# Second loop of an eight-layer kernel: the next pair's residual input prepared one iteration ahead

## The reference

```python
x = x + _L0_attn_ref(_layernorm(x), ...)   # cosine-weighted attention and an MLP
x = x + _L0_ffn_ref(_layernorm(x), ...)    # channel mix with the token before
x = x + _L1_attn_ref(_layernorm(x), ...)   # latent attention
x = x + _L1_ffn_ref(_layernorm(x), ...)    # two groups of 32 experts, 2 chosen in each
x = x + _L2_attn_ref(_layernorm(x), ...)   # rotary causal attention, 16 heads
x = x + _L2_ffn_ref(_layernorm(x), ...)    # 8 experts, 2 chosen
x = x + _L3_attn_ref(_layernorm(x), ...)   # state-space layer (Mamba), gated RMS norm
x = x + _L3_ffn_ref(_layernorm(x), ...)    # attention among the heads of a token, soft experts
```

## Time and profile before

| | |
|---|---|
| median of 3 runs | 5831.26 us (5829.92 to 5835.9) |
| profiled execution, its time | 5804.77 us |
| its span | 5803.2 us |
| second loop | from 2543.4 us to 5661.5 us of the span |
| busy PE, DVE, POOL, ACT | 4503.4, 3665.5, 2279.9, 1757.0 us |
| mean granted TensorE clock | 0.862 |

### The profile page before, as it was taken

The page is one execution under the profiler, slowest core; times in us unless marked ns, Lnnn a source line. Parts: engine busy times, 40 slices in busy tenths (PEclk is TensorE's granted clock), DMA queues, the critical chain, the costliest instruction groups (busy, mean ns, idle before and its releaser), DMA issues. The chain is left out here.

```text
span 5803.2 us, 89650 instructions
## 1 busy us (share of the span) xinstructions
PE 4503.4 (78%) x33608; PEld 2606.0 (45%) x33608; DVE 3665.5 (63%) x10873; ACT 1757.0 (30%) x2749; POOL 2279.9 (39%) x2754
## 2 busy tenths in 40 slices
PE   5979788797979795958778688787786786877872
PEld 4454445454544443634535435445354354453442
DVE  4565656565656563647586685676765956757665
ACT  2424243333333342423232241232322422413220
POOL 3333333333342334445253271362533623614435
PEclk9989899898989897968888888888888888888885
DMA  3000000000000004720000000000000000000000
GB/s 119 8 16 12 13 13 13 15 11 16 10 20 6 19 7 159 231 72 2 16 14 5 18 8 10 21 2 16 14 5 16 10 9 20 4 13 17 5 14 4
DMA packets 141739, 145.74 MB, mean 25 GB/s; under 512 B 31112, under 2 KB 126026, under 8 KB 140770
## 3 DMA queue, kind: packets, MB, share of 16 engines
q1 hardware_dynamic: 114130, 93.01, 5.5%
q0 software_dynamic: 18432, 37.79, 2.3%
q10 hardware_dynamic: 8736, 8.91, 0.5%
HBM read 69.17 MB, written 62.59 MB: 23 GB/s over the span
## 5 line engine op out<-in xcount | busy, mean ns | idle before, releaser
L815 DVE CUSTOM_DVE_ANT_0 twin<-twin,w_mask_row 128x512 f32<-128x512 f32 (+3 forms) x2048 | 951.5, 522 | 335.4 <-PE twin L1777 333.9
L1777 PE MATMUL twin<-arena 32*128 32x128 f32 (+3 forms) x4096 | 803.5, 519 | 38.9 <-DMA arena<-hres 16.7
L1795 PE MATMUL twin<-arena 32*128 32x128 f32 (+3 forms) x4096 | 792.6, 505 | 33.7 <-DVE arena L815 32.1
L1723 PE MATMUL twin<-w_ident_b 128*128 128x512 bf16 x1536 | 455.1, 449 | 390.3 <-DVE mv L775 158.6
L1450 ACT ACTIVATE arena<-twin 128x768 f32<-128x768 f32 (+1 forms) x544 | 479.3, 881 | 686.6 <-PE twin L1806 387.5
L705 POOL TENSOR_SCALAR ve<-mv 128x4 f32<-128x4 f32 x128 | 27.5, 214 | 1458.9 <-DVE mv L775 1458.3
L1795 PEld LDWEIGHTS twin<-arena 32*128 32x128 f32 x4096 | 348.3, 199 | 479.4 <-issue 289.2
L328 POOL DMA_INDIRECT got<-sorted_y,back x288 | 280.8, 975 | 540.4 <-ACT ring L1657 290.5
L1723 PEld LDWEIGHTS twin<-w_ident_b 128*128 128x128 bf16 x1536 | 155.9, 111 | 660.3 <-DVE mv L775 182.1
L1777 PEld LDWEIGHTS twin<-arena 32*128 32x128 f32 x4096 | 356.9, 206 | 198.1 <-issue 111.2
L320 POOL DMA_INDIRECT sorted_x<-got,w_mo_first_slots x288 | 287.0, 997 | 97.9 <-issue 56.0
(11 more groups left out here) (422 smaller groups left out, 9473.4 us busy)
## 6 DMA issues: line engine op xcount, KB each, us to landing
sorted_y<-arena SPq DMA_DIRECT2D x96, 256.0 KB, 2.8
sorted_x<-zeros ACTq DMA_DIRECT2D x2, 4096.0 KB, 19.9
a<-sorted_x SPq DMA_DIRECT2D x64, 128.0 KB
b<-sorted_x SPq DMA_DIRECT2D x64, 128.0 KB, 2.5
hres<-sorted_x SPq DMA_DIRECT2D x64, 128.0 KB
sorted_x<-got,w_mo_first_slots POOLq DMA_INDIRECT x288
got<-sorted_y,back POOLq DMA_INDIRECT x288, 2.6
x_out<-w_l_w SPq DMA_DIRECT2D x18, 256.0 KB, 2.3
```

The source lines that it names most:

```text
L815: last = dve.tensor_tensor_reduce(s[:, e, at:at + w], s[:, e, at:at + w], W["mask_row"][:, T - w:T], -1.0, 3e38, ALU.add, ALU.min, into)
L1723: pe.matmul(into, ident_b, ident_b.unsqueeze(1).broadcast_to([P, NT, P]), start=True, stop=True, skip_group_check=True)
L1777: last = pe.matmul(s[:, e, at:at + w], queries[r, P * i:P * (i + 1)], keys[r, 0:w], start=(at == 0), stop=True, skip_group_check=True)
L1795: last = pe.matmul(s[:, e, at:at + w], keys[r, P * m:P * (m + 1)], queries[r, P * m:T], start=(at == 0), stop=(tag == "l2"), skip_group_ch ...
```

## The change

The next pair's residual input gets a buffer of its own, `XN[q]`, and the head of an iteration is moved into the end of the one before.

- SP no longer loads X at the start of an iteration. It loads `XN[q]` for the next pair once DVE has read the present one (`l2_moved`, after the attention). `kept_x` gets one more row for the index of the iteration after the last.
- The additions (`add_chosen`, the same 16 instructions for each q) are cut into four steps and placed by hand: steps 0 to 2 of q = 0 before the wait for the output projection, the rest, both statistics and both norms into `l3_front` around the two `take_queries`. Every iteration does them, the last too, whose result nobody uses.
- The expert section does them for the first pair, behind its row fetches.
- ACT's four fills move from the head to the start of `l3_front` (`clear_rows`), and into the expert section for the first iteration.
- POOL's fetches are two after each `l3_xc`, two after each of four and one after each of four more `l3_decay` signals, none in the head front. It makes the two scales at the end of the iteration.
- PE's `keep_busy` at the head of the iteration is gone, and its turns wait for nothing.
- `back`, the table of rows and weights, is loaded at once at the start, no longer behind the additions.

```diff
+        XN = pair_sb("x_next", [P, NT, D])
...
+        def add_chosen(dve, sg, q, steps):
+            for c in steps:
+                k, g = divmod(c, GROUPS)
+                if c == 0:
+                    dve.wait_ge(sg[f"x_loaded{q}"], 16)
+                    dve.wait_ge(sg[f"m_got{q}"], 16 * SLOTS_OF_SEQ)
+                else:
+                    dve.wait_ge(sg[f"m_adding{q}"], c)
+                for t in range(NT):
+                    n = NT * GROUPS * k + GROUPS * t + g
+                    i = dve.scalar_tensor_tensor(XN[q][:, t], got[q][:, n],
+                                                 back[:, q, SLOTS_OF_SEQ + n:SLOTS_OF_SEQ + n + 1], XN[q][:, t],
+                                                 ALU.mult, ALU.add)
+                i.then_inc(sg[f"m_adding{q}"], 1)
+                if c == ADDS - 1:
+                    dve.wait_ge(sg[f"m_adding{q}"], ADDS)
+        def clear_rows(act, q):
+            act.activation(at_k4[q], ...)      # ones
+            return act.activation(at_q4[q], ...)   # zeros
...
 # expert section, DVE (POOL makes the two scales, ACT clears the rows)
+                        for q in PAIR:
+                            add_chosen(dve, sg, q, range(ADDS))
+                            ... statistics of XN[q] ...
+                        for q in PAIR:
+                            dve.wait_ge(sg["rstd_ready"], q + 1)
+                            ... A[q] = norm of XN[q] ...
...
 # second loop, SP
-                        for q in PAIR if first < LAYERS else ():
-                            src = (x_in[...] if first == 0 else kept_x[bass.ds(pair + 1, 1), q])
+                        for q in PAIR if first == 0 else ():
+                            src = x_in[...]
                             sp.dma_start(X[q][:], src).then_inc(sg[f"x_loaded{q}"], 16)
...
-                            sp.wait_ge(sg[f"l2_rows_clear{q}"], 2)
...
+                        for q in PAIR if first <= L2_ATTENTION < last else ():
+                            src = kept_x[bass.ds(pair + 2, 1), q]...
+                            sp.wait_ge(sg["l2_moved"], q + 1)
+                            sp.dma_start(XN[q][:], src).then_inc(sg[f"x_loaded{q}"], 16)
...
 # POOL
-                                        fetch_rows(pool, sg, (4 + m,))
+                                        fetch_rows(pool, sg, (4 + 2 * m, 5 + 2 * m))
...
-                                        fetch_rows(pool, sg, (12 + 2 * m, 13 + 2 * m))
+                                        fetch_rows(pool, sg, (20 + 2 * m, 21 + 2 * m) if m < 4 else (24 + m,))
...
-                                if layer == LAYERS - 1:
-                                    fetch_rows(pool, sg, (28 + 2 * of_layer, 29 + 2 * of_layer))
...
 # DVE
                         def l2_attention():
-                            for q in PAIR:
-                                add_experts(q)
-                                layernorm_stats(q)
-                            for q in PAIR:
-                                layernorm_apply(q, "l2_a")
...
-                                done(dve.tensor_tensor(X[q][:], X[q][:], l2_bo, ALU.add))
+                                dve.tensor_tensor(X[q][:], XN[q][:], l2_bo, ALU.add).then_inc(sg["l2_moved"], 1)
...
                                 rms_apply(q, ma_y[q], ma_y[q], "l3_y")
+                            add_chosen(dve, sg, 0, range(0, ADDS - 1))
                             for q in PAIR:
                                 dve.wait_ge(sg["l3_out_mm"], q + 1)
...
+                            add_chosen(dve, sg, 0, range(ADDS - 1, ADDS))
+                            layernorm_stats(0, XN)
+                            add_chosen(dve, sg, 1, range(0, 2))
+                            take_queries(0)
+                            layernorm_apply(0, "l2_a", src=XN)
+                            add_chosen(dve, sg, 1, range(2, ADDS))
+                            layernorm_stats(1, XN)
+                            take_queries(1)
+                            layernorm_apply(1, "l2_a", src=XN)
...
 # ACT
-                            fill(at_k4[0], 1, "l2_rows_clear0")
-                            fill(at_q4[0], 0, "l2_rows_clear0")
-                            fill(at_k4[1], 1, "l2_rows_clear1")
-                            to_f(0, "l2_turn", 1, "l2_f", b=3)
-                            fill(at_q4[1], 0, "l2_rows_clear1")
-                            to_f(1, "l2_turn", 2, "l2_f", b=3)
+                            for q in PAIR:
+                                to_f(q, "l2_turn", q + 1, "l2_f", b=3)
...
                         def l3_front():
+                            for q in PAIR:
+                                act.wait_ge(sg["l3_out_mm"], q + 1)
+                                clear_rows(act, q)
...
 # PE
                         def l2_attention():
-                            keep_busy(pb(0, 3), ("m_added", 1), ("stats_ready", 1), ("m_added", 2), ("stats_ready", 2))
                             for q in PAIR:
-                                turn(q, A[q], "l2_a", q + 1, "l2_turn", b=3)
+                                turn(q, A[q], None, 0, "l2_turn", b=3)
```

More of the change, by code:

```diff
@@ L329, in fetch_rows @@
                                         bass.IndirectOffsetOnAxis(ap=back[:, q, n:n + 1].bitcast(U32), axis=0)
-                                        ).then_inc(sg["m_got"], 16)
+                                        ).then_inc(sg[f"m_got{q}"], 16)
+        def add_chosen(dve, sg, q, steps):
[15 more added lines that the diff above has]
+        def clear_rows(act, q):
+            act.activation(at_k4[q], W["l2_rope_k"].unsqueeze(1).broadcast_to([P, HG, T]), ACT.Identity,
+                           bias=W["ones"][:, 0:1], scale=0.0)
+            return act.activation(at_q4[q], W["l2_rope_k"].unsqueeze(1).broadcast_to([P, HG, T]), ACT.Identity,
+                                  bias=0.0, scale=0.0)
         for first, last in PARTS:
@@ L466, in _ @@
                                                ).then_inc(sg["e_silu"], 1)
+                        act.wait_ge(sg["e_w"], 2 * UNITS)
+                        for i in range(3):
+                            act.wait_ge(sg[f"e_stored{i}"], 16 * (UNITS // 3))
+                        for q in PAIR:
+                            clear_rows(act, q)
                     @block.vector
@@ L547, in _ @@
                         dve.tensor_copy(back[:], ex_back[:, 2:4]).then_inc(sg["e_first_back"], 1)
+                        for q in PAIR:
+                            add_chosen(dve, sg, q, range(ADDS))
+                            for t in range(NT):
+                                i = dve.bn_stats(BS[q][:, t], XN[q][:, t])
+                            done(i)
+                            for t in range(NT):
+                                i = dve.bn_aggr(MV[q][:, t], BS[q][:, t])
+                            i.then_inc(sg["stats_ready"], 1)
+                        for q in PAIR:
+                            dve.wait_ge(sg["rstd_ready"], q + 1)
+                            for t in range(NT):
+                                dve.tensor_scalar(A[q][:, t], XN[q][:, t], MV[q][:, t, 0:1], RS[q][:, t:t + 1],
+                                                  ALU.subtract, ALU.mult)
                 clear_signals()
@@ L555, in _ @@
                     def _(sp):
-                        for q in PAIR if first < LAYERS else ():
-                            src = (x_in[bass.ds(pair, 1), q] if first == 0 else kept_x[bass.ds(pair + 1, 1), q]
-                                   ).rearrange("b (t p) d -> p (b t) d", p=P)
+                        for q in PAIR if first == 0 else ():
+                            src = x_in[bass.ds(pair, 1), q].rearrange("b (t p) d -> p (b t) d", p=P)
                             sp.dma_start(X[q][:], src).then_inc(sg[f"x_loaded{q}"], 16)
@@ L1367, in l3_front, with take_queries @@
                                                        W["l3f_bo"].unsqueeze(1).broadcast_to([P, NT, D]), ALU.add))
-                            for q in PAIR:
+                            def take_queries(q):
                                 dve.wait_ge(sg["f_q_mm"], q + 1)
@@ L1583, in l2_attention @@
                         def l2_attention():
-                            def fill(rows4, value, ready):
-                                act.activation(rows4, W["l2_rope_k"].unsqueeze(1).broadcast_to([P, HG, T]), ACT.Identity,
-                                               bias=W["ones"][:, 0:1] if value else 0.0, scale=0.0
-                                               ).then_inc(sg[ready], 1)
-                            fill(at_k4[0], 1, "l2_rows_clear0")
-                            fill(at_q4[0], 0, "l2_rows_clear0")
-                            fill(at_k4[1], 1, "l2_rows_clear1")
-                            to_f(0, "l2_turn", 1, "l2_f", b=3)
-                            fill(at_q4[1], 0, "l2_rows_clear1")
-                            to_f(1, "l2_turn", 2, "l2_f", b=3)
```

(6 more changed lines are left out.)

63 lines of the change are left out of this document (30 added, 33 removed).

## The result

The change takes the median from 5830.59 to 5778.94 us, four runs each on one chip: ratio 0.991, 95% interval 0.989 to 0.9929. The forecast was 5776, in a range of 5750 to 5808.

A forecast was written before the change was run, and what follows sets the result against it. It took the serial chain at each turn between iterations, 28.4 us from last work to first scores, as the bound. Seven turns 53.9 plus first iteration 4.4 minus last 3.3 gave 55 us, median 5831.3 to 5776, range 5750 to 5808.

The forecast's parts named there:

- the clock term: Turn to first scores: without keep-busy PE starts at 1.2 GHz, costing 2.5 us a turn, bounds 0 to 5.
- DVE's wait for the load: Head of the iteration: DVE idles 103.4 us in eight waits for X to arrive, 12.9 us an iteration.
- turn behind the start of PE's branch: Loop turn: PE's turn of q = 0 starts 3.8 us after its branch began instead of 17.3, removing 13.5 us.
- DVE's tail behind ACT: Iteration's end: DVE ends at 2939.0 against ACT's 2935.75, so the turn comes 3.3 us later.
- saved in a turn: Each of seven turns with a branch back: 13.5 - 3.3 - 2.5 = 7.7 us saved, 53.9 in all.
- twelve additions under the output projection: DVE before the output projection's wait: 3.5 us of additions hidden in 3.80 us of idle time, no cost.
- first iteration, last fetch to scores: Entry without a branch: first scores at 2565.1 instead of 2569.56, 4.4 us saved.
- A low clock that drags on: Attention: five or more of eight iterations lose 3.5 us, 18 to 28 us, giving 5794 to 5804; chance 0.17.
- slower by the same mechanism: Low clock lasts further into iterations; 19 us more each eats the gain, 30 gives 5862 us; chance 0.07.
- The larger saving: Turn: short branch and no clock cost give 5730 us; long branch without clock cost 5759; chance 0.16.
- Nothing changes: Turn: uncovered additions (3.5), longer branch (1.4) and low clock throughout (2.5) take 7.4 of 7.7 us, 5831; chance 0.05.
- The profiled time: Whole profiled execution: forecast to go from 5804.8 to 5750 us.

The follow-up runs named there:

- e8: Changed kernel with the twelve additions of q = 0 moved from before the output projection's wait into `l3_front`; ratio 0.9936 to the kernel before, 5747.32 us.
- e6: Changed kernel with two pairs in one step of the second loop, three branches back instead of seven; ratio 0.986 to the kernel before, 5709.82 us.
- e5: Changed kernel with keep-busy matmuls added at the end of PE's `l3_front`; ratio 0.9909 to the kernel before, 5737.04 us.
- e3: Kernel before without the keep-busy matmuls at the head of the second loop's iterations; ratio 1.0036 to the kernel before, 5857.65 us.
- e4: Changed kernel run again, unchanged; ratio 0.987 to the kernel before, 5768.2 us.
- e11: Changed kernel run a third time, unchanged; ratio 0.9898 to the kernel before, 5726.64 us.
- e2: Kernel before with only the next pair's residual input loaded one iteration ahead into its own buffer; ratio 0.9954 to the kernel before, 5813.07 us.
- e10: e7 with all eight pairs written out, no branch back in the second loop; ratio 0.9793 to the kernel before, 5672.10 us.
- e9: e7 with two pairs in one step of the second loop; ratio 0.9799 to the kernel before, 5668.35 us.
- e7: Changed kernel with q = 0 additions moved into the last four scan steps, q = 1's before the output projection's wait; ratio 0.9857 to before, 5699.43 us.
- e1: Kernel before run again, unchanged; ratio 1.0, 5837.46 us.

## Why the prediction was right

Its mechanism held step by step for the turn, and so did the sum. Two things in it were not as told: what the clock term holds, and what DVE's wait for the load was.

| term | forecast | measured | from |
|---|---|---|---|
| turn behind the start of PE's branch | 3.8 us | 3.6 | after, mean of 7 (before: 17.5) |
| DVE's tail behind ACT | 3.3 | 3.6 | turn shown |
| turn to scores, more than before | 2.5 | 3.0 | 9.1 to 12.1, mean of 7 |
| saved in a turn | 7.7 | 7.3 | ACT's end to scores, 28.3 to 21.1, mean of 7 |
| twelve additions under the output projection | 0 | 0 | 0.41 us idle left; e8: 3.5 each turn without the cover |
| first iteration, last fetch to scores | -4.4 | -5.9 | 30.1 to 24.2 |
| whole | -55 | -52 to -70 | three pairs of medians; -60 in the rest of the span |

The terms as measured add up to 7 x 7.3 + 5.9 - 3.6 = 53 us, the last for DVE's tail in the last iteration. About 5 of the 60 us in the rest are in no term: the profiles of after have 1.7 iterations in the slow form in the mean, those of before three.

**The branch.** PE's rows were the ones to believe. After a branch back PE is away for 3.33 to 3.85 us, DVE's record of 0.07 says nothing of it, and e6 takes the wait away by taking the branch away. The Trainium skill, "Advanced Engine Details and Errata", section "Control Flow Timing", gives about 0.108 us; the measurement on PE differs by a factor of thirty and decides. Its page "Runtime: NRT & Kernel Launch", section "Instruction fetch mechanics", prefers unrolled code for this reason, and e6 agrees in its direction (0.986 against 0.9909 for e5 in the same group). The stall for a fetch, which the prediction took from this section, fits the traces too: in the seven turns of after PE's branch ends 1.34 to 1.37 us behind a 16 KB packet of the instruction queue. That PE waits for just this packet is read from the timing; no run changed the packet alone.

**The clock.** The term of 2.5 us was nearly right in size (3.0 measured) and wrong in what it holds. The low clock costs 1.7 to 1.9 us (e6 without branch 10.8 and e3 11.0, against 9.1), and the other 1.3 us are PE's second lateness behind the branch, at the keys, which no row of before could show: there PE stood in keep-busy at that time. That the two together come near the forecast is partly luck. In the first iteration, without a branch, turn to scores took 11.6 us (11.1 and 10.9 in e4 and e11) where 13.1 were reckoned, which is most of what that entry gained beyond the forecast.

**DVE's load wait.** The prediction read the 7.83 us of the earlier trace rows as a wait for the transfer. e2 shows that with the load already there DVE still starts 2.8 us after its branch. For the sum it made no difference, since after the change DVE's first work is the bias of the keys, 8.6 us behind POOL's first memset.

**The rivals.** *A low clock that drags on* did not come with the change: the slow form of the first thirteen exponentials is taken in three of eight iterations in both profiles of before, in one, three and one of eight in the three of after. With it falls *slower by the same mechanism* for this change. The effect itself exists: the slow form has a mean grant of 0.68 to 0.71 where the others have 0.73 to 0.81, and it is taken in five of eight in e3 and six of eight in e10. What decides it is not shown. *The larger saving* needed a short branch or no clock cost; both costs are there, and only e9 and e10 get near 0.98. Its sum also leaves out the 3.3 us lost in the last iteration. *Nothing changes* needed three bounds at once, and none was reached.

**The profiled time** was the miss: 5750 was expected, and the span is 5781.4. The first loop makes it, 33.8 us longer in the one profile than in the other. The same difference of 55 us, taken from the median, held.

Open: why the first loop moves between 2209 and 2278 us with the same code, and what puts an iteration of the second loop into the slow form.

## What to carry to other kernels

A loop's end with barriers is serial time of the whole core: work that depends on nothing in the next iteration belongs in front of it, under a wait that is there, and the last engine before the barrier sets the price (0.29 us an addition outside the cover, nothing inside it). Look at what every engine does after the branch, not at the length of its branch record. Writing out two iterations per step was worth as much here (e6) as moving the rest of the tail under cover (e7), and writing out all eight gave no more that could be measured. When two profiles are compared, cut the span at the loops first and leave out the stretch whose code is the same; then separate the turns from the iterations between them.

## What the runs showed of the hardware

- PE's branch back took 3.3 to 3.9 us in after (up to 5.3 in e1), 0.08 where the loop is left. After it the turn ran, and the next instructions were late again by 1.3 us (e6: keys 3.06 to 3.30 us after the turn against 1.77).
- PE's branch ended 1.34 to 1.37 us after the end of a 16 KB packet of the instruction queue q8, the keys started 1.24 to 1.46 us after the end of the next one (after, seven turns). In the longest branch of before, 5.1 us, a q8 packet took 2.3 us, in after's seven turns 1.0 to 1.5.
- DVE's branch record is 0.07 us, but the first instruction behind it came 2.8 to 3.8 us later (e2).
- After 5.1 us without matmuls, right behind 4.2 us of back-to-back ones, the granted clock was 0.50 (e5). After 2.1 us of idle time it was still up for the turn in five of seven turns, and fell while PE was at work on the keys (e10).
- The way from the first scores to the fourteenth exponential took 44.1 to 45.1 us at a mean grant of 0.73 to 0.81, or 47.8 at 0.68 to 0.71, in the same code.
- The same first loop took 2209 to 2278 us in thirteen profiles, and the kernel before had medians of 5788 to 5839 us in the three groups. Only ratios on one chip, or the rest of the span, resolve what this study measures.
